# Expert tiles of one expert's 128 rows, and tiles of 64 rows of each of two experts in two column groups

## The reference

```python
logits = x @ gate_weight.T                       # x: 1024 tokens x 256
probs = jax.nn.softmax(logits, axis=-1)          # 64 experts
routing_weights, selected_experts = lax.top_k(probs, 8)
routing_weights = routing_weights / routing_weights.sum(-1, keepdims=True)
combine = zeros((T, 64)).at[arange(T)[:, None], selected_experts].add(routing_weights)
for wgu, wd, we in experts:                      # wgu: 256 x 192, wd: 96 x 256
    gate, up = split(x @ wgu, 2)
    final += we[:, None] * ((silu(gate) * up) @ wd)
```

## Time and profile before

| | us |
|---|---|
| median of 3 runs | 536.47 (535.07 to 536.64) |
| the profiled execution | 533.95 |
| its span in the trace | 532.2 |
| PE busy in the span | 476.5 (90%) |
| DVE busy | 352.1 (66%) |
| ACT busy | 332.1 (62%) |
| POOL busy | 240.1 (45%) |

### The profile page before, as it was taken

One profiled execution on the slowest core, in us unless ns is written; L12 is line 12 of the kernel. 1 busy time (PEld: TensorE's weight loads), 2 busy tenths in 40 slices (PEclk: granted clock), 3 DMA queues, 4 the chain that ended last, 5 costly groups with the idle time before them and its releaser, 6 DMA issues.

```text
span 532.2 us, 10363 instructions
## 1 busy us (share of the span) xinstructions
PE 476.5 (90%) x2751; PEld 386.7 (73%) x2751; DVE 352.1 (66%) x1175; ACT 332.1 (62%) x1021; POOL 240.1 (45%) x255
## 2 busy tenths in 40 slices
PE   3886999999989799999998657999999999999975
PEld 1466767787778777778775535889999899998722
DVE  5968587487398489479679743866566666665443
ACT  4557786788676879777987713555555555555500
POOL 0344111011012571102577777767667676675710
PEclk9899999999999999999999859999999999999989
DMA  8930993000020220200276245999999999995397
GB/s 281 420 128 20 292 333 99 1 0 1 2 79 10 72 74 9 79 2 1 81 264 272 101 141 166 357 400 401 399 391 391 396 399 398 393 371 177 92 383 283
DMA packets 65416, 108.54 MB, mean 204 GB/s; under 512 B 10234, under 2 KB 41159, under 8 KB 64976
## 3 DMA queue, kind: packets, MB, share of 16 engines
q1 hardware_dynamic: 56192, 90.93, 48.0%
q0 software_dynamic: 9168, 16.95, 8.7%
HBM read 81.31 MB, written 34.77 MB: 218 GB/s over the span
## 4 chain that ended last, share of the span: by engine, by line
PE 60%; ACT 14%; DVE 14%; DMA 6%; issue 4%; POOL 1%; POOLq 0%; SPq 0%; DVEq 0%; ACTq 0%
PE ps L1474 15%; PE ps L1494 10%; PE ps L1214 10%; PE ps L1339 7%; ACT lg L634 5%; ACT lg L577 3%; DVE lg L912 2%; DMA pairs<-pair_rows 2%; PE ps L1255 2%; PE ps L1210 2%; PE ps L1212 2%; PE ps L1211 2%; PE ps L1262 2%; PE ps L1320 2%; PE ps L1295 2%
## 5 line engine op out<-in xcount | busy, mean ns | idle before, releaser
L563 POOL DMA_INDIRECT pair_rows<-eout,dest x127 | 126.6, 997 | 55.6 <-DVE dest L1185 44.1
L1474 PE MATMUL ps<-wts,xg 128*128 128x192 f32 x508 | 105.2, 330 | 0.0
L1474 PEld LDWEIGHTS ps<-wts,xg 128*128 128x128 f32 x508 | 81.0, 193 | 0.1
L774 ACT ACTIVATE sact<-ps 128x96 f32<-128x96 f32 x127 | 31.9, 251 | 76.5 <-PE ps L1474 76.5
L1494 PE MATMUL ps<-wts,aT 96*128 96x256 f32 x254 | 76.0, 381 | 0.0
L1182 DVE COPY xg<-ps 128x256 f32<-128x256 f32 x127 | 53.9, 424 | 29.8 <-PE ps L1214 28.8
L634 ACT ACTIVATE lg<-lg,mneg 128x128 f32<-128x128 f32 (+1 forms) x128 | 56.4, 443 | 26.3 <-DVE mneg L912 26.3
L1195 DVE SCALAR_TENSOR_TENSOR aact<-sact,xrow,ps 128x96 f32<-128x96 f32 x127 | 39.8, 314 | 48.4 <-ACT sact L774 48.0
L483 POOL DMA_INDIRECT slot_rows<-rows,pair_slot x48 | 48.5, 1011 | 32.9 <-DVE hit L977 20.3
L577 ACT ACTIVATE eout<-ps 128x256 f32<-128x256 f32 x127 | 48.8, 384 | 17.2 <-PE ps L1494 1.2
L1214 PE MATMUL ps<-ident,xrow 128*128 128x128 f32 x254 | 50.1, 278 | 10.1 <-DMA xrow<-slot_rows 10.1
(11 more groups left out here) (220 smaller groups left out, 1041.0 us busy)
## 6 DMA issues: line engine op xcount, KB each, us to landing
wts<-in_experts_dram SPq DMA_DIRECT2D x127, 320.0 KB, 9.1
xrow<-slot_rows SPq DMA_DIRECT2D x127, 130.0 KB
slot_rows<-zero SPq DMA_DIRECT2D x1, 8320.0 KB, 28.4
pairs<-pair_rows SPq DMA_DIRECT2D x16, 512.0 KB, 8.1
wT<-in_wq_t_dram SPq DMA_DIRECT2D x4, 512.0 KB, 6.7
wq_raw<-in_wq_l_dram SPq DMA_DIRECT2D x1, 2048.0 KB, 14.7
wo_sb<-in_wo_l_dram SPq DMA_DIRECT2D x1, 2048.0 KB, 20.6
bm<-bias_rows SPq DMA_DIRECT2D x4, 512.0 KB, 3.6
```

Source lines behind the costliest of these rows:

```text
L563: nc.gpsimd.indirect_dma_start(out=pair_d, out_offset=bass.IndirectOffsetOnAxis(ap=dest[:, t:t + 1], axis=0), in_=eout[t % NOUT][:], in_of ...
L1474: ins = nc.tensor.matmul(ps[:, 2 + u % 2, 0:I2], xg[u % 3][:, cc, :], wts[u % NBUF][:, cc * I2:(cc + 1) * I2], start=(cc == 0), stop=(cc = ...
```

## The change

A tile is now 64 rows of an expert, and two such half tiles of two experts form a *double*: rows 0 to 63 on partitions 0 to 63, the other's on 64 to 127. The 64 first half tiles make 32 doubles (`FIXED`), and 128 further half tiles make 64 (`EXTRA`), so that the loop runs over 96 doubles: 28 fixed, 64 extra, 4 fixed. The two transposes, the activation's transpose, all work of VectorE and ScalarE and the scatter are done for both halves together. The matmuls with weights are done for each half by itself: the stationary operand has 64 columns, and the result goes to PSUM partitions 0 to 63 or 64 to 127, that is to one of two column groups of the array. Doubles are taken two at a time (`GROUPS`) after the first four, which share each copy and silu.

All experts' weights are kept in SBUF (160 KB of each partition), loaded once in 16 parts of 4 experts (`load_kept`). Parts 0 to 3 are loaded where the first 16 tiles' weights were, 4 to 6 at three points up to the end of attention, 7 to 10 behind the rows of doubles 0 to 3, 11 to 15 behind the rows of doubles 5 to 9 and behind the table of further tiles. In an extra double, the first half reads the kept weights at an address from a register (`off_of`); the second half reads a copy of its expert's weights, which SyncE loads for it into one of eight buffers, gate and up (192 KB) and down (96 KB) by separate DMAs. The rows of a double are two DMAs of 64 rows. The activation buffers `sact`, `aact`, `aT` are single now, the table arrays are 64 x 15, three constants are made earlier on GpSimd, and its descriptor area is set to 4096 bytes.

```diff
-            def load_wts(t, e):
-                if t >= NBUF:
-                    sp.wait_ge(dn_done, t - NBUF + 1)
-                sp.dma_start(wts[t % NBUF][:], experts[e].rearrange("e p n -> p (e n)")).then_inc(wts_ld[t % NBUF], 16)
+            def load_kept(i):
+                if i >= NLD:
+                    sp.wait_ge(wts_ld[i % NLD], 16 * PER)
+                for e in range(i * PER, (i + 1) * PER):
+                    sp.dma_start(wts[:, e * EW:(e + 1) * EW], experts[e]).then_inc(wts_ld[i % NLD], 16)
+            def load_rows(d, first):
+                if d >= NROW:
+                    sp.wait_ge(act_ready, group_of[d - NROW] + 1)
+                    sp.wait_ge(dest_ready, group_of[d - NROW] + 1)
+                for h in range(2):
+                    sp.dma_start(xrow[d % NROW][h * R:(h + 1) * R], slot_d[first[h], :]).then_inc(rows_ld[d % NROW], 16)
+            def load_copy_gu(m, r):
...
+                sp.dma_start(copy_gu[m % NCOPY][:], experts[bass.ds(r // CAP, 1), :, 0:CC * I2].rearrange("e p n -> p (e n)")
+                             ).then_inc(copy_gu_ld[m % NCOPY], 16)
+            def load_copy_dn(m, r):
...
+            for d in range(NDBL + 4):
+                if d < NDBL:
...
+                        if d < TOPK // 2:
+                            sp.wait_ge(last_sent[2 * d], 16 * len(LAST))
+                            sp.wait_ge(last_sent[2 * d + 1], 16 * len(LAST))
...
+                if d < 4:
+                    load_kept(7 + d)
+                if d == 5:
+                    sp.wait_ge(rows_ready, 1)
+                if 5 <= d < 10:
+                    load_kept(6 + d)
+                m = d - 2 - FIRST_EXTRA
+                if 0 <= m < EXTRA:
...
+                    load_copy_gu(m, base_of[m][1])
+                m = d - 4 - FIRST_EXTRA
+                if 0 <= m < EXTRA:
+                    load_copy_dn(m, base_of[m][1])
...
-                    for cc in range(CC):
-                        ins = nc.tensor.matmul(ps[:, 2 + u % 2, 0:I2], xg[u % 3][:, cc, :], wts[u % NBUF][:, cc * I2:(cc + 1) * I2],
-                                               start=(cc == 0), stop=(cc == CC - 1))
+                    for cc in range(CC):
+                        for h in range(2):
+                            if j < FIXED:
+                                w = (2 * j + h) * EW + cc * I2
+                                moving = wts[:, w:w + I2]
+                            elif h == 0:
+                                moving = wts[:, bass.ds(off_of[m] + cc * I2, I2)]
+                            else:
+                                moving = copy_gu[m % NCOPY][:, cc * I2:(cc + 1) * I2]
+                            ins = nc.tensor.matmul(ps[h * R:(h + 1) * R, 2 + u % 2, k * I2:(k + 1) * I2],
+                                                   xg[u % 2][:, k, cc, h * R:(h + 1) * R], moving, start=(cc == 0), stop=(cc == CC - 1))
```

More of the change, by code:

```diff
@@ L85, in adaln_attn_ffn @@
         ident = at("ident", [P, P], take(512))
-        small = take(2 * KIB)
+        small = take(2 * KIB + 256)
         so = [small]
@@ L201, in adaln_attn_ffn @@
[L201 to L208, removed]
@@ new lines, in adaln_attn_ffn @@
+        t_off = at("t_off", [P, MORE // 2], take(256), I32)
+        assert o <= 24 * KIB
+        o = spare
+        t_rows = at("t_rows", [P, MORE], take(512), I32)
+        row_size = (RW * 4 + 31) // 32 * 32
+        xrow = [at(f"xrow{i}", [P, RW], take(row_size) if i < 3 else (i - 3) * row_size) for i in range(NROW)]
+        assert (NROW - 3) * row_size <= 8 * KIB
+        copy_gu = [at(f"copy_gu{i}", [P, CC * I2], r3 + i * CC * I2 * 4) for i in range(NCOPY)]
+        copy_dn = [at(f"copy_dn{i}", [P, C], r3 + 12 * KIB + i * KIB if i < 4 else row_off + (i - 4) * KIB if i < 7 else take(KIB))
+                   for i in range(NCOPY)]
@@ L388, in _ @@
+            sp.wait_ge(h2_full, NB)
+            sp.wait_ge(out_done, NB + TB)
+            load_kept(5)
+            load_kept(6)
             for i in range(2):
                 sp.wait_ge(sent[i], sent_ahead(LAST[i]))
[L390 to L407, removed]
@@ new lines, in _ @@
+            base_of = {}
+            for d in range(NDBL + 4):
+                if d < NDBL:
+                    j = SEQ[d]
+                    if j < FIXED:
+                        if d < TOPK // 2:
+                            sp.wait_ge(last_sent[2 * d], 16 * len(LAST))
+                            sp.wait_ge(last_sent[2 * d + 1], 16 * len(LAST))
+                        if d == 3:
+                            sp.wait_ge(x2_turned, NTB // 2)
+                        load_rows(d, [slice((2 * j + h) * CAP, (2 * j + h) * CAP + R) for h in range(2)])
+                    else:
+                        m = j - FIXED
+                        if m % 4 == 0:
+                            _, r8 = nc.values_load_multi_w_load_instructions(
+                                t_rows[0:1, 2 * m:2 * m + 8], engines=[SP_ENGINE], min_val=0, max_val=NE * CAP - R,
+                                skip_runtime_bounds_check_because="each is 0 or an expert's base plus at most its row count less one tile")
+                            for k in range(4):
+                                base_of[m + k] = r8[2 * k:2 * k + 2]
+                        load_rows(d, [bass.ds(r, R) for r in base_of[m]])
+                if d < 4:
[6 more added lines that the diff above has]
+                if 0 <= m < EXTRA:
+                    if m == 0:
+                        for i in range(3):
+                            sp.wait_ge(scattered[i], 16)
+                    load_copy_gu(m, base_of[m][1])
+                m = d - 4 - FIRST_EXTRA
+                if 0 <= m < EXTRA:
+                    load_copy_dn(m, base_of[m][1])
@@ new lines, in down @@
+            def down(a):
+                for k, d in enumerate(GROUPS[a]):
+                    j = SEQ[d]
+                    if j >= FIXED:
+                        m = j - FIXED
+                        pe.wait_ge(copy_dn_ld[m % NCOPY], 16 * (m // NCOPY + 1))
+                    for h in range(2):
+                        if j < FIXED:
+                            w = (2 * j + h) * EW + CC * I2
+                            moving = wts[0:I, w:w + C]
+                        elif h == 0:
+                            moving = wts[0:I, bass.ds(off_of[m] + CC * I2, C)]
+                        else:
+                            moving = copy_dn[m % NCOPY][0:I, :]
+                        ins = nc.tensor.matmul(ps[h * R:(h + 1) * R, 6 + a % 2, k * C:(k + 1) * C], aT[0:I, k, h * R:(h + 1) * R], moving,
+                                               start=True, stop=True)
+                ins.then_inc(dn_done, 1)
```

368 lines of the change are left out of this document (227 added, 141 removed).

## The result

The changed kernel took 618.32 us (median of four runs, 615.21 to 625.12) beside 535.96 us for the kernel before: a ratio of 1.153, with a 95% interval of 1.149 to 1.157. I had forecast 581, with a range of 540 to 640. One of the four runs, the 625.12, was in the chip's slower state; the median of the other three is 616.95, so a difference of 1 or 2 us from this kernel says nothing. The profiled execution took 615.21 us, with a span of 613.4.

A forecast was written before the change was run, and what follows sets the result against it. TensorE bound the kernel before, SyncE's issues the extras after: first down copy at 386.6, 63 steps of 2.40 less 2.1 to 535.7, end to 576.7, 1.8 outside the span, 2.5 to the median: 581 us, range 540 to 640.

The forecast's parts named there:

- PE bounds the kernel before, SyncE the one after: Expert loop: TensorE sets 1.41 us a tile before; SyncE's DMA issues pace the 64 extra doubles after, 154 us.
- SyncE per extra double, 2.40 us: Extra doubles: four DMA issues at 0.565 us plus 0.54 / 4 for reading the table, without waits.
- My lower end: SyncE in extra doubles: 0.44 us a DMA if halves or copies were cheaper, 32.5 us less in all.
- TensorE per double, 1.60 with slots A1 A2 B1 B2: Matmuls with weights: the column groups overlap partly, n MATMULs taking n/2 + 1 slots; 3.21 us for two doubles with transposes.
- The registers' 0.24 us a double: PE in extra doubles: one register computation exposed at each matmul block's start, raising 1.60 to 1.84 us a double.
- rival 1: Matmuls with weights: column groups do not overlap and PE sets the pace, 2.50 us a double; 623 us, chance 0.24.
- Its far end: Column groups not overlapping, with all register cost exposed on PE: 664 us; chance 0.06.
- Its clock form: PE in extra doubles: the clock falls to the 1.2 GHz level, 1.60 becomes 3.2 us a double; 632 us.
- Fill: Before the extras' pace: double 3's rows issued at 327.4, doubles 10 and 11 turned at 358, first down copy at 386.6.
- End: After the extras: last down copy at 535.7, first read of `pair_rows` at 545.0, then 31.7 us to the span's end.
- rival 3: Extra doubles: SyncE hides altogether and the halves overlap perfectly, 1.41 us a double; faster, 519 us, chance 0.09.
- its no-change form: Extra doubles: SyncE hidden with PE at 1.60 us a double; 536 us, no change; chance 0.03.

The follow-up runs named there:

- the halves apart: Changed kernel with each group's gate-up and down products issued all of column group 0 first, then all of column group 1: 623.10 us, ratio 1.162.
- the later parts: Changed kernel with one copy DMA a double issued by ScalarE, and kept parts 7 to 15 issued behind later doubles, up to 21: 546.00 us.
- Runs of two: The 546.00 us kernel with gate-up products issued two in a row for one column group instead of alternating one by one: 546.66 us, ratio 1.021.

## Why the prediction was right, and where its size was off

- *PE bounds the kernel before, SyncE the one after.* Right, and shown: taking one issue a double off SyncE gave 30 us, taking both off gave 62, with the DMAs and TensorE filling up as it went.
- *SyncE per extra double, 2.40 us.* The step that was mis-sized: 2.78. Two halves take 1.37 and not 1.13, the copies 1.16 and not 1.13, long issues add 0.11; 0.38 x 63 = 24 us of the 37. I had taken a 64-row issue for "the same form" as a 128-row one, and the trace of before had no row of it. From the first copy of a down part to the last this makes 174.8 us for my 149.1. My lower end, 0.44 an issue if halves were cheaper, was on the wrong side altogether; no upper end above 0.565 was given. The Trainium skill (DMA: Bandwidth & Descriptors, Rules for kernel authors) had the rule that I set aside as one on bandwidth, one DMA over 128 partitions and not two over halves; here it costs 71 us in the kernel before, and by the issuing engine's time.
- *TensorE per double, 1.60 with slots A1 A2 B1 B2.* 1.56 without waits, but not by my reasoning. Gate and up take 1.35 us for 1.46, down 0.97 for 1.09, the transposes 0.80 for 0.66; the pairs overlap whole. Against 0.66 + 8 x 0.1625 + 4 x 0.2175 = 2.83 us a group, 0.29 are left for everything else. The drain at a change of tiling mode (the Trainium skill, TensorEngine Tiling (Array Packing), Key Properties) must lie in these 0.29, for two changes a group. The registers' 0.24 us a double was nothing: the kernel after can't show it, since PE waited for rows there, but in the run with the copies on ScalarE groups of extra doubles take the same 3.12 as fixed ones. The premise that starts are in order across column groups was wrong too, as the halves apart show. It cost nothing where the halves alternate.
- *Column groups don't overlap (rival 1, 623 us).* Wrong by mechanism, though its number lay within 5 us of the result. A time alone would have confirmed the wrong story. The weight loads that it feared are shorter with 64 columns, 137 ns for gate and up (median) where 128 columns took 190. Its far end should read 661 and not 664, by its own terms. Its clock form didn't matter: over windows of the extra doubles the granted clock was 0.79 to 0.87 on average, so partly at the 1.2 and mostly at the 2.4 GHz level, and 1.00 where PE was busy for 38.56 of 40 us (above). In the kernel after it cost nothing there, since SyncE set the pace and waited for nobody.
- *Fill.* Double 3's rows were issued at 331.73, not 327.4, and doubles 10 and 11 turned at 366.45, not 358. I had taken 327.4 from the kernel before, with the scatter ahead of it landing in 3.19 us. In the kernel after the last scatter is issued at 325.39 and lands at 331.68, so it took 6.3. Here SyncE waited 5.0 us for it, and then 4.7 for the table, before the parts behind could start: 
```profile
SPq L452 <- DMA slot_rows<-rows,pair_slot: 5.0, 1, 5.0
SPq L411 <- DVE t_rows L1257: 4.7, 1, 4.7
```

  The first copy of a down part came at 396.81 for 386.6: 10 us. That kept parts in flight hold the last scatters up is likely, but was not tested by itself.
- *End.* From the last copy of down to the first read of `pair_rows` 11.9 us for 9.3, and 29.9 from there for 31.7. Right. With the fill's 10.2 and the extras' 25.7 these make up all of the 36.7 us by which the profiled execution passed my 578.5.
- *Faster (rival 3, 519; 536 for its no-change form).* It asked for SyncE hidden. With it hidden the kernel takes 556, and 546 with the later parts. I put PE's 1.60 into that sum but not the DMA engines, which are full at 1.71, nor the fill.

## What to carry to other kernels

Count the DMAs that one queue must issue per unit of work, and price them by a row of the very shape: here an engine that computes nothing set the pace of 175 us. TensorE did two half tiles in two column groups at nearly the price of one whole tile (1.56 us for 1.41). But the halves had separate rows and weights, so two DMAs a tile became four a double, and the saving was out of reach. Before giving up a 128-row transfer for two of 64, look whether the issuing engine has the time. Merging the two copies brought 30 of the 82 us back, and a second queue, here ScalarE's, another 32.

## What the hardware showed that I had not expected

- A DMA of 64 rows takes its issuing queue longer than one of 128 with the same bytes (0.55 and 0.43 us on fixed addresses, 0.48 and 0.33 on computed ones), and slows a 128-row one behind it (0.58 and 0.45). Neighbouring or alternate rows make no difference.
- The two column groups of TensorE take their instructions in order each for itself, and one started ahead of three older MATMULs of the other. Runs of two cost 0.02 us a double against strict alternation, runs of eight 0.35 on top of 1.56. Register computations between the MATMULs cost nothing.
- A DMA share of about 1.04 stood for 386 GB/s in the kernel before and for 328 in the run with the copies on ScalarE. With half columns for rows it was 0.95 at 297:

```profile
330.00:530.00 200.00, 177.53 (x1052) 143.41 (x1050) 104.89 (x364) 92.59 (x350) 116.39 (x118) 1.00 0.95 297
```

So bandwidth is to be judged by the share, not by the GB/s.
